# Node by node with four graphs innermost: another column order in a graph kernel on one core

## The chip, the cores and the metric

The kernel runs on one core of one Trainium2 chip. The metric is the device time of one execution in microseconds; lower is better.

## What is computed

64 graphs of 128 nodes with 128 features each go through two layers, each with a layer norm, a ReLU and a residual. The first layer has a convolution branch along the nodes (1 tap, then 17 taps), a message branch whose weights come from distances of three projected values, and a GRU-like gate over both. The second is a plain graph convolution. Cut to what matters:

```python
h = relu(layernorm(x))                                  # per node
c = relu(bn1(conv1(h)));  x_conv = relu(bn2(conv17(c)) + h)
s = h @ w_se.T + b_se                                   # 3 values a node
A = exp(-|s_n - s_m|^2) * adj
x_nmp = A @ relu(h @ w_msg.T + b_msg)
gi = [x_conv, x_nmp] @ w_ih.T + b_ih;  gh = h @ w_hh.T + b_hh
r, z = sigmoid(gi_r + gh_r), sigmoid(gi_z + gh_z)
x = x + (1 - z) * tanh(gi_n + r * gh_n) + z * h
x = x + adj @ (relu(layernorm(x)) @ weight) + bias
```

## The kernel before

The graphs are handled in 16 groups of four (`GG = 4`, `W = 512` columns), two groups being a pair (8 graphs, `CG`). Most of the first layer is kept transposed: features on the 128 partitions, and the 512 (node, graph) columns of a group along the free dimension. In those tiles (`hT`, `h_hi`, `h_lo`, `n_hi`, `n_lo`, `zh`, `cand`) the columns stand graph by graph, 128 nodes of one graph in a row. The nodes of a graph are loaded in an order by phase: `PH = 4` phases of `QN = 32` nodes, so that the convolution of 17 taps splits into products with inputs of one phase each.

`x_turn(g)` (L285) turns the four normalised graphs `hn` into PSUM with four transposes; ScalarE writes `h_hi` (rounded to fp32r) and `hT` from there, VectorE the rest `h_lo`. `conv1(g)` (L296) is one product of 512 columns, whose result ScalarE writes to `c1` (L567), laid out as [phase, graph of the pair, 36], two zeros at either end of the 32 nodes. `pre` (L756, on GpSimd) forms differences of phases in `ac` and `px` (a fast-convolution scheme with nine products in place of sixteen); ScalarE and VectorE split them into `cx_hi` (L537) and `cx_lo` (L862). `product` (L266) then runs, for each of the four or five taps `j` of one of nine inputs, three matmuls of 256 columns (`split_product`: L262, L263, L264) on `cx[:, x, :, j:j + QN]`, that is, eight runs of 32 numbers that start `j` numbers into a row of 36.

```python
last = split_product(acc[:, side * CG * QN:(side + 1) * CG * QN],
                     conv_hi[:, w * D:(w + 1) * D], conv_lo[:, w * D:(w + 1) * D],
                     cx_hi[:, x, :, j:j + QN], cx_lo[:, x, :, j:j + QN], ...)
```

`messages(g)` (L307) multiplies `hT` of one graph (the stationary operand) with `w_ms` (131 columns), after a bias matmul for each two graphs (L318); as an fp32 matmul each becomes two instructions at L320, with a weight load each. `neighbour_sums(g)` (L340) is for each graph the product of `msg` and `att`, again two instructions each. `gates_h`, `gates_n`, `gates_c` (L352 to L385) are 27 matmuls of 512 columns for each group. `o_turn(g)` (L390) turns the blend `zh` (stationary) back to nodes on partitions, in four transposes. The rest (`adj_h2`, `layer2`) works on nodes by partition.

Nothing is scheduled automatically. Every engine has its list of work written out: an `opening()`, and then `step(t)` for t = 1 to 8, in which TensorE alternates the parts for the two groups a, b of the next pair (turn, conv1, messages, distances, sums), the nine products of this pair, and the parts for the groups pp, qq of the pair before; then come the gates. A middle step begins with `x_turn(a)`, `o_turn(pp)`, the product of input `X22`, `conv1(a)` (which waits for `h_lo` of a), `messages(a)`, `x_turn(b)`, the product of `X12`, `o_turn(qq)`, `conv1(b)` (which waits for `h_lo` of b), `messages(b)`. In step 7 there is no next pair, so no `x_turn`, `conv1` and `messages`; step 8 has the last two groups' ends alone.

## Time and profile before

| | us |
|---|---|
| median of 3 runs (lowest, highest) | 382.32 (381.64, 383.23) |
| the profiled execution, whole time | 385.51 |
| its span in the profile | 383.4 |
| TensorE busy in the span | 345.2 |
| VectorE busy | 285.2 |
| ScalarE busy | 208.3 |
| GpSimd busy | 175.4 |

The span goes from the first to the last instruction of the core; the execution's whole time is 2.1 us more. In the rows below PE is TensorE's matmuls and PEld its weight loads, DVE is VectorE, ACT ScalarE, POOL GpSimd. A busy share counts the time in which an instruction of the engine is under way. Matmuls are pipelined: one starts before the last has ended, so their durations add to more than the time that passes, and what one costs the stream is read from start to start. In the timeline, equal instructions in a row are merged to one line with their number (x4), and the time in it is that of all of them.

### The profile page before, as it was taken

The page shows a single profiled execution, that of the slowest core. Times are in us where ns is not written, and L with a number is a line of the kernel's source. Part 1 is how long each engine was busy: PE and PEld are TensorE (multiplying, and loading weights), DVE is VectorE, ACT ScalarE, POOL GpSimd, SP SyncE. Part 2 cuts the span into 40 slices and gives each one's busy share as a digit, 9 for nine tenths or more (in the row PEclk, how much of TensorE's full clock was granted, in tenths as well). Part 3 has the DMA queues.
Part 4 walks back from the last instruction along what each step waited for, and adds up shares of the span by engine and source line. Part 5 has one row for each costly group of instructions (what it writes and reads, how often), then busy time and mean ns, then how long its engine had stood idle before and what let it go on. Part 6 is the DMA issues. An engine that isn't in the chain of part 4 may idle for free.

```text
span 383.4 us, 6302 instructions
## 1 busy us (share of the span) xinstructions
PE 345.2 (90%) x2196; PEld 314.9 (82%) x2196; DVE 285.2 (74%) x736; ACT 208.3 (54%) x402; POOL 175.4 (46%) x140
## 2 busy tenths in 40 slices
PE   7777956979999899999999999989999999989935
PEld 7776856759998899889987999889988998989725
DVE  3596878778877997698878887798758976743571
ACT  1545823485854586548745785458545835261422
POOL 7762336211890369224952298028901592153031
PEclk9875989998999999999999999999999999999955
DMA  7600020000130013000210031002100010000001
GB/s 257 264 3 0 0 85 0 0 3 0 57 109 2 1 41 122 6 0 30 100 39 1 2 110 56 0 2 68 44 1 2 0 57 0 3 29 27 0 0 56
DMA packets 7807, 15.10 MB, mean 39 GB/s; under 512 B 992, under 2 KB 1376, under 8 KB 7648
## 3 DMA queue, kind: packets, MB, share of 16 engines
q1 hardware_dynamic: 7488, 14.56, 10.9%
q8 instruction: 18, 0.29, 0.3%
q10 hardware_dynamic: 288, 0.14, 0.1%
q14 instruction: 13, 0.11, 0.1%
HBM read 10.50 MB, written 4.19 MB: 38 GB/s over the span
## 4 chain that ended last, share of the span: by engine, by line
issue 45%; POOL 32%; DVE 9%; PE 7%; ACT 5%; DMA 1%; SPq 0%; POOLq 0%; ACTq 0%; DVEq 0%
POOL work L1116 5%; POOL rs L1074 4%; POOL ac L769 3%; POOL base L1126 3%; POOL base L1128 3%; POOL px L773 3%; POOL base L1132 2%; POOL px L771 2%; POOL px L766 2%; POOL rs L1069 2%; DMA x_ring<-x_in 1%; ACT hn L548 1%; POOL px L763 1%; DVE cx_lo L862 1%; DVE st L786 1%
## 5 line engine op out<-in xcount | busy, mean ns | idle before, releaser
L1074 POOL TENSOR_TENSOR rs<-ve,neg_half 128x4 f32<-128x4 f32 x16 | 16.2, 1010 | 98.7 <-DVE ve L903 98.7
L262 PE MATMUL pP<-cx_hi,conv_hi 128*128 128x256 f32 x176 | 54.2, 308 | 4.1 <-DVE cx_lo L862 4.1
L264 PE MATMUL pP<-cx_hi,conv_lo 128*128 128x256 f32 x176 | 52.0, 296 | 0.0
L263 PE MATMUL pP<-cx_lo,conv_hi 128*128 128x256 f32 x176 | 52.0, 295 | 0.0
L262 PE MATMUL pQ<-cx_hi,conv_hi 128*128 128x256 f32 x144 | 46.0, 319 | 4.1 <-issue 3.6
L1069 POOL TENSOR_TENSOR rs<-ve,neg_half 128x8 f32<-128x8 f32 (+1 forms) x9 | 16.4, 1825 | 63.6 <-DVE ve L793 63.6
L263 PE MATMUL pQ<-cx_lo,conv_hi 128*128 128x256 f32 x144 | 43.2, 300 | 0.0
L264 PE MATMUL pQ<-cx_hi,conv_lo 128*128 128x256 f32 x144 | 43.2, 300 | 0.0
L262 PEld LDWEIGHTS pP<-cx_hi,conv_hi 128*128 128x128 f32 x176 | 34.1, 194 | 4.4 <-issue 2.5
L596 ACT ACTIVATE work<-work,nb,rs 128x128 f32<-128x128 f32 x64 | 26.3, 483 | 15.0 <-DVE nb L907 15.0
L862 DVE TENSOR_TENSOR cx_lo<-px,cx_hi 128x576 fp32r<-128x576 f32 x32 | 34.0, 1082 | 0.6 <-ACT cx_hi L537 0.6
L264 PEld LDWEIGHTS pP<-cx_hi,conv_lo 128*128 128x128 f32 x176 | 34.2, 194 | 0.0
L263 PEld LDWEIGHTS pP<-cx_lo,conv_hi 128*128 128x128 f32 x176 | 34.2, 194 | 0.0
L262 PEld LDWEIGHTS pQ<-cx_hi,conv_hi 128*128 128x128 f32 x144 | 28.9, 201 | 4.8 <-issue 3.7
L1116 POOL TENSOR_TENSOR work<-work,late 128x512 f32<-128x512 f32 x16 | 23.1, 1442 | 14.8 <-DVE pair L838 11.2
L263 PEld LDWEIGHTS pQ<-cx_lo,conv_hi 128*128 128x128 f32 x144 | 28.9, 201 | 0.0
L264 PEld LDWEIGHTS pQ<-cx_hi,conv_lo 128*128 128x128 f32 x144 | 28.9, 201 | 0.0
L923 DVE SCALAR_TENSOR_TENSOR xc_lo<-base,xc_hi 128x512 fp32r<-128x512 f32 x16 | 17.1, 1068 | 12.8 <-ACT xc_hi L606 12.8
L616 ACT ACTIVATE work<-pNR,rz_b 128x512 f32<-128x512 f32 x16 | 11.0, 687 | 26.4 <-PE pNR L264 26.4
L853 DVE TENSOR_TENSOR att<-att,adj_ring 128x512 f32<-128x512 f32 x16 | 23.6, 1474 | 1.7 <-ACT att L587 1.3
L548 ACT ACTIVATE hn<-x_ring,nb,rs 128x128 f32<-128x128 f32 x56 | 22.3, 483 | 1.6 <-DVE nb L799 1.6
L537 ACT ACTIVATE cx_hi<-px 128x576 fp32r<-128x576 f32 x32 | 20.8, 676 | 2.3 <-POOL px L763 2.3
(233 smaller groups left out, 1018.0 us busy)
## 6 DMA issues: line engine op xcount, KB each, us to landing
x_ring<-x_in SPq DMA_DIRECT2D x16, 256.0 KB, 2.6
adj_ring<-adj_in SPq DMA_DIRECT2D x16, 256.0 KB, 3.1
out<-x_ring SPq DMA_DIRECT2D x16, 256.0 KB, 2.0
work<-conv_in SPq DMA_DIRECT2D x1, 1088.0 KB, 7.7
x_ring<-gate_in SPq DMA_DIRECT2D x1, 576.0 KB, 8.0
work<-bias_in SPq DMA_DIRECT2D x1, 132.0 KB, 7.6
early<-early_in SPq DMA_DIRECT2D x1, 129.5 KB, 3.2
late<-late_in ACTq DMA_DIRECT2D x1, 128.0 KB, 3.4
```

Source lines behind the costliest of these rows:

```text
L262: pe.matmul(acc, w_hi, m_hi, start=start, stop=False)
L263: pe.matmul(acc, w_hi, m_lo, start=False, stop=False)
L264: return pe.matmul(acc, w_lo, m_hi, start=False, stop=stop)
L537: act.activation(cx_hi[:, CX_PARTS[k][0]:CX_PARTS[k][1]], cx_source(k), ACT.Copy).then_inc(cxhi_set, 1)
L548: last = act.activation(graph(hn[g % 2], j), xs(g, j), ACT.Identity, bias=nb1[:, i:i + 1], scale=rs1[:, i:i + 1])
L596: last = act.activation(graph(h2[g % 2], j), graph(x1[g % 2], j), ACT.Relu, bias=nb2[g % 2][:, j:j + 1], scale=rs2[g % 2][:, j:j + 1])
L853: dve.tensor_tensor(att[g % 2], att[g % 2], adjs(g), ALU.mult).then_inc(att_set, 1)
L862: dve.tensor_tensor(cx_lo[:, part], cx_source(k), cx_hi[:, part].bitcast(F32), ALU.subtract)\
L923: dve.scalar_tensor_tensor(xc_lo[:, 2 * e:2 * e + 2], base[e][:], 0.0, xc_hi[:, 2 * e:2 * e + 2].bitcast(F32), ALU.max, ALU.subtract)\
L1069: pool.tensor_tensor(rs1[:, lane], ve1[:, lane], neg_half[:, lane], ALU.pow).then_inc(rs1_set, 1)
L1074: pool.tensor_tensor(rs2[g % 2][:], ve2[g % 2][:], neg_half[:, 0:GG], ALU.pow).then_inc(rs2_set, 1)
L1116: pool.tensor_tensor(x1[g % 2].rearrange("p (g d) -> p g d", g=GG), x1[g % 2].rearrange("p (g d) -> p g d", g=GG), l1_bias, ALU.add).then_ ...
```

## The change

The columns of a group are kept node by node, with the four graphs innermost: column 4n + j is node n of graph j (`lane(t, j)` picks graph j in steps of four). `x_turn` and `neighbour_sums` write their results to PSUM in steps of four; `messages` and `o_turn` read their stationary operand in steps of four. `c1`, `ac`, `px`, `cx_hi`, `cx_lo` become [phase or input, group of the pair, 144], with the pads of eight numbers at either end, and a tap `j` starts `4 * j` numbers into the row, in two runs of 128. `xc_hi`, `xc_lo` and `base` hold each group's columns together. The order of the instructions and their number are the same on all engines.

```diff
--- before.py
+++ after.py
@@ -17,7 +17,8 @@
 TAPS = 17
 PH = 4
 QN = N // PH
-QP = QN + 4
+QW = QN * GG
+QR = (QN + 4) * GG
 EPS = 1e-5
 S = 3
 MS = D + S
@@ -94,17 +95,17 @@
         n_hi = [sb(f"n_hi{i}", [128, 2 * W], F32R) for i in range(2)]
         n_lo = [sb(f"n_lo{i}", [128, 2 * W], F32R) for i in range(2)]
 
-        c1 = sb("c1", [128, PH, CG, QP])
-        ac = sb("ac", [128, 2, CG, QP])
-        px = sb("px", [128, 8, CG, QP])
-        cx_hi = sb("cx_hi", [128, 9, CG, QP], F32R)
-        cx_lo = sb("cx_lo", [128, 9, CG, QP], F32R)
+        c1 = sb("c1", [128, PH, 2, QR])
+        ac = sb("ac", [128, 2, 2, QR])
+        px = sb("px", [128, 8, 2, QR])
+        cx_hi = sb("cx_hi", [128, 9, 2, QR], F32R)
+        cx_lo = sb("cx_lo", [128, 9, 2, QR], F32R)
         s22 = sb("s22", [128, CG * QN])
         s12 = sb("s12", [128, CG * QN])
         s32 = sb("s32", [128, CG * QN])
-        base = [sb(f"base{i}", [128, 2, CG, QN]) for i in range(2)]
-        xc_hi = sb("xc_hi", [128, PH, CG, QN], F32R)
-        xc_lo = sb("xc_lo", [128, PH, CG, QN], F32R)
+        base = [sb(f"base{i}", [128, 2, 2, QW]) for i in range(2)]
+        xc_hi = sb("xc_hi", [128, PH, 2, QW], F32R)
+        xc_lo = sb("xc_lo", [128, PH, 2, QW], F32R)
 
         sq = sb("sq", [128, GG, S])
         sv = sb("sv", [128, GG, S + 1])
@@ -188,6 +189,9 @@
 
         def graph(t, j):
             return t[:, j * N:(j + 1) * N]
+
+        def lane(t, j):
+            return t.rearrange("p (n g) -> p g n", g=GG)[:, j]
 
         def turn_bank(g):
             return pI if g == 1 else pF
@@ -267,7 +271,7 @@
                 for j, w in enumerate(weights):
                     last = split_product(acc[:, side * CG * QN:(side + 1) * CG * QN],
                                          conv_hi[:, w * D:(w + 1) * D], conv_lo[:, w * D:(w + 1) * D],
-                                         cx_hi[:, x, :, j:j + QN], cx_lo[:, x, :, j:j + QN],
+                                         cx_hi[:, x, :, j * GG:j * GG + QW], cx_lo[:, x, :, j * GG:j * GG + QW],
                                          start=j == 0, stop=j == len(weights) - 1)
                 return last
 
@@ -290,7 +294,7 @@
                 elif g > 1:
                     have(pe, hlo_set, g)
                 for j in range(GG):
-                    last = pe.transpose(graph(turn_bank(g), j), graph(hn[g % 2], j), ident[:])
+                    last = pe.transpose(lane(turn_bank(g)[:], j), graph(hn[g % 2], j), ident[:])
                 last.then_inc(hT_placed, 1)
 
             def conv1(g):
@@ -317,7 +321,7 @@
                 for i in range(2):
                     pe.matmul(ms[:, 2 * i:2 * i + 2, 0:MP], ones_r[:], bias_r[:], start=True, stop=False)
                     for j in range(2 * i, 2 * i + 2):
-                        last = pe.matmul(ms[:, j, 0:MS], graph(half(hT, g), j), w_ms, start=False, stop=j % 2 == 1)
+                        last = pe.matmul(ms[:, j, 0:MS], lane(half(hT, g), j), w_ms, start=False, stop=j % 2 == 1)
                 last.then_inc(ms_done, 1)
 
             def rows_turn(g):
@@ -346,7 +350,7 @@
                 elif g > 1:
                     have(pe, nlo_set, g)
                 for j in range(GG):
-                    last = pe.matmul(graph(rows_bank(g), j), graph(msg[g % 2], j), graph(att[g % 2], j), start=True, stop=True)
+                    last = pe.matmul(lane(rows_bank(g)[:], j), graph(msg[g % 2], j), graph(att[g % 2], j), start=True, stop=True)
                 last.then_inc(nmp_done, 1)
 
             def gates_h(g):
@@ -377,9 +381,7 @@
 
             def gates_c(g):
                 have(pe, xclo_set, g + 2 - g % 2)
-                j = slice(g % 2 * GG, (g % 2 + 1) * GG)
-                m_hi = xc_hi[:, :, j].rearrange("p k g m -> p g k m")
-                m_lo = xc_lo[:, :, j].rearrange("p k g m -> p g k m")
+                m_hi, m_lo = xc_hi[:, :, g % 2], xc_lo[:, :, g % 2]
                 gate_part(pR, 0, 0, m_hi, m_lo, False, True).then_inc(r_done, 1)
                 gate_part(pI[:], 0, 2, m_hi, m_lo, False, True).then_inc(i_done, 1)
                 gate_part(z_bank(g)[:], 0, 1, m_hi, m_lo, False, True).then_inc(z_done, 1)
@@ -395,7 +397,7 @@
                     have(pe, v_set, g + 1)
                 bank = pI if g % 2 else pH
                 for j in range(GG):
-                    last = pe.transpose(graph(bank, j), graph(zh[g % 2], j), ident[:])
+                    last = pe.transpose(graph(bank, j), lane(zh[g % 2], j), ident[:])
                 last.then_inc(o_placed, 1)
 
             def adj_h2(g):
@@ -563,9 +565,7 @@
                 if g % 2 == 0:
                     have(act, pre_set, 5 * (g // 2) - 2)
                     have(act, cxlo_set, 5 * (g // 2) - 4)
-                j = slice(g % 2 * GG, (g % 2 + 1) * GG)
-                act.activation(c1[:, :, j, 2:2 + QN].rearrange("p k g m -> p g k m"),
-                               conv1_bank(g)[:].rearrange("p (g k m) -> p g k m", g=GG, k=PH), ACT.Relu,
+                act.activation(c1[:, :, g % 2, 2 * GG:2 * GG + QW], conv1_bank(g)[:].rearrange("p (k w) -> p k w", k=PH), ACT.Relu,
                                bias=bn_b[:, 0:1], scale=bn_a[:, 0:1]).then_inc(c1_set, 1)
 
             def messages(g):
@@ -760,18 +760,18 @@
                 have(eng, pre_set, 5 * t + 3)
             have(eng, cxlo_set, 5 * t)
             if k == 1:
-                last = eng.tensor_tensor(px[:, X12:X21 + 1], c1[:, 1:3], c1[:, 3:4].to_broadcast([128, 2, CG, QP]),
+                last = eng.tensor_tensor(px[:, X12:X21 + 1], c1[:, 1:3], c1[:, 3:4].to_broadcast([128, 2, 2, QR]),
                                          ALU.subtract)
             elif k == 2:
-                last = eng.tensor_tensor(px[:, X32:X23 + 1, :, 0:QP - 1], c1[:, 0:3:2, :, 1:QP],
-                                         c1[:, 3:4, :, 0:QP - 1].to_broadcast([128, 2, CG, QP - 1]), ALU.subtract)
+                last = eng.tensor_tensor(px[:, X32:X23 + 1, :, 0:QR - GG], c1[:, 0:3:2, :, GG:QR],
+                                         c1[:, 3:4, :, 0:QR - GG].to_broadcast([128, 2, 2, QR - GG]), ALU.subtract)
             elif k == 3:
-                last = eng.tensor_tensor(ac[:], c1[:, 0:2], c1[:, 2:3].to_broadcast([128, 2, CG, QP]), ALU.subtract)
+                last = eng.tensor_tensor(ac[:], c1[:, 0:2], c1[:, 2:3].to_broadcast([128, 2, 2, QR]), ALU.subtract)
             elif k == 4:
                 last = eng.tensor_tensor(px[:, X11:X31 + 1], ac[:], px[:, X12:X32 + 1:2], ALU.subtract)
             else:
-                last = eng.tensor_tensor(px[:, X13:X33 + 1, :, 0:QP - 1], ac[:, :, :, 1:QP],
-                                         px[:, X12:X32 + 1:2, :, 0:QP - 1], ALU.subtract)
+                last = eng.tensor_tensor(px[:, X13:X33 + 1, :, 0:QR - GG], ac[:, :, :, GG:QR],
+                                         px[:, X12:X32 + 1:2, :, 0:QR - GG], ALU.subtract)
             last.then_inc(pre_set, 1)
 
         @block.vector
...
@@ -1117,7 +1117,7 @@
                                    l1_bias, ALU.add).then_inc(x1b_set, 1)
 
             def own(t, e):
-                phases = hT[t % 2][:].rearrange("p (g k m) -> p k g m", g=CG, k=PH)
+                phases = hT[t % 2][:].rearrange("p (h k w) -> p k h w", h=2, k=PH)
                 return phases[:, 2 * e:2 * e + 2]
 
             def sums(t):
...
```

## Rows read from the trace of the kernel before

**Rows 1.** The page: busy time by engine, and TensorE's granted clock in 40 slices.

```profile
PE 345.2 (90%) x2196; PEld 314.9 (82%) x2196; DVE 285.2 (74%) x736; ACT 208.3 (54%) x402; POOL 175.4 (46%) x140
...
PEclk9875989998999999999999999999999999999955
```

**Rows 2.** Busy time by stretch of the middle, with count, clock and DMA.

```profile
core 0: us, PE busy (x) PEld busy (x) DVE busy (x) ACT busy (x) POOL busy (x), PEclk, DMA share, GB/s
130.00:170.00 40.00, 38.82 (x263) 35.60 (x262) 33.19 (x88) 24.90 (x50) 20.98 (x14) 1.00 0.12 40
...
sum 200.00, PE 195.54 PEld 179.52 DVE 161.15 ACT 121.95 POOL 100.87; mean PE 39.11 PEld 35.90 DVE 32.23 ACT 24.39 POOL 20.17
```

**Rows 3.** TensorE's timeline in a middle step: `X12`, then `o_turn(qq)`, `conv1(b)`.

```profile
253.88 0.28 PE L263 MATMUL pP<-cx_lo,conv_hi 128*128 128x256 f32 x1
...
254.11 0.29 PE L262 MATMUL pP<-cx_hi,conv_hi 128*128 128x256 f32 x1
...
255.29 0.28 PE L262 MATMUL pP<-cx_hi,conv_hi 128*128 128x256 f32 x1
...
255.65 0.60 PE L398 MATMUL pI<-ident,work 128*128 128x128 f32 x4
256.57 0.50 PE L262 MATMUL pH<-h_hi,early_hi 128*128 128x512 f32 x1 [0.33 <-DVE h_lo L813]
```

**Rows 4.** TensorE's timeline: bias matmul and messages of a; gates on n, xc, next group.

```profile
252.19 0.28 PE L318 MATMUL pNR<-bias_r,ones_r 128*128 128x264 f32 x1
252.31 0.61 PE L320 MATMUL pNR<-early,hT 128*128 128x131 f32 x4
...
278.13 0.40 PE L262 MATMUL pNR<-n_hi,gate_hi 128*128 128x512 f32 x1
...
280.23 0.40 PE L262 MATMUL pNR<-xc_hi,gate_hi 128*128 128x512 f32 x1
...
282.33 0.39 PE L262 MATMUL pNR<-h_hi,gate_hi 128*128 128x512 f32 x1
```

**Rows 5.** The opening at the lower clock: stretch, then TensorE's product of `X21`.

```profile
33.00:36.00 3.00, 3.00 (x15) 3.00 (x15) 2.13 (x4) 2.25 (x7) 0.00 (x0) 0.50 0.00 0
...
33.60 0.41 PE L262 MATMUL pQ<-cx_hi,conv_hi 128*128 128x256 f32 x1
...
35.52 0.41 PE L262 MATMUL pQ<-cx_hi,conv_hi 128*128 128x256 f32 x1
```

**Rows 6.** Groups by shape (busy us, mean ns); L320 by itself (min/median/max); sums (timeline).

```profile
L262 PE MATMUL pP<-cx_hi,conv_hi 128*128 128x256 f32 x176 | 54.2, 308 | 4.1 <-DVE cx_lo L862 4.1
...
L262 PE MATMUL pQ<-cx_hi,conv_hi 128*128 128x256 f32 x144 | 46.0, 319 | 4.1 <-issue 3.6 <-DVE conv_lo L867 0.5
...
L320 PEld LDWEIGHTS pNR<-early,hT 128*128 128x128 f32 x128 | 18.6, 204 | 0.7
...
L398 PEld LDWEIGHTS pI<-ident,work 128*128 128x128 f32 x32 | 4.0, 151 | 3.2 <-DVE work L885 3.2
...
L320 PE MATMUL pNR<-early,hT x8: 273/275/275, 252.3 to 253.2; 128*128 128x131 f32 x8
...
272.07 1.06 PE L349 MATMUL pF<-att,msg 128*128 128x128 f32 x8
```

**Rows 7.** TensorE's timeline: two waits of the opening, and `conv1(a)` in a middle step.

```profile
20.09 0.36 PE L262 MATMUL pP<-cx_hi,conv_hi 128*128 128x256 f32 x1 [2.30 <-DVE cx_lo L862]
...
26.77 0.36 PE L262 MATMUL pP<-cx_hi,conv_hi 128*128 128x256 f32 x1 [1.76 <-DVE cx_lo L862]
...
250.29 0.28 PE L264 MATMUL pP<-cx_hi,conv_lo 128*128 128x256 f32 x1
251.41 0.47 PE L262 MATMUL pH<-h_hi,early_hi 128*128 128x512 f32 x1 [0.84 <-DVE h_lo L813]
```

**Rows 8.** Groups by shape of ScalarE and GpSimd that the change touches.

```profile
L567 ACT ACTIVATE c<-pH,bn_b,bn_a 128x512 f32<-128x512 f32 x15 | 11.7, 782 | 15.7 <-PE pH L264 15.7
...
L1126 POOL TENSOR_TENSOR base<-base,hT 128x512 f32<-128x512 f32 x8 | 13.0, 1623 | 13.0 <-DVE base L931 13.0
```

More of the change, by code:

```diff
@@ L917, in conv_out @@
                 have(dve, (sumE_set, sumO_set)[e], t + 1)
-                dve.scalar_tensor_tensor(base[e][:], (pQ, pP)[e][:].rearrange("p (s g m) -> p s g m", s=2, g=CG),
+                dve.scalar_tensor_tensor(base[e][:], (pQ, pP)[e][:].rearrange("p (s h w) -> p s h w", s=2, h=2),
                                          bn_a[:, 1:2], base[e][:], ALU.mult, ALU.add).then_inc(ct_set, 1)
@@ L930, in between @@
                 have(dve, xclo_set, 2 * t)
-                dve.scalar_tensor_tensor(base[1][:].rearrange("p s g m -> p s (g m)"),
+                dve.scalar_tensor_tensor(base[1][:].rearrange("p s h w -> p s (h w)"),
                                          pQ[:].rearrange("p (s w) -> p s w", s=2), bn_a[:, 1:2],
@@ L1057, in _ @@
             pool.memset(ones_r[:].bitcast(F32), 1.0).then_inc(rows_zero, 1)
-            pool.memset(px[:, X32:X23 + 1, :, QP - 1:QP], 0.0)
-            pool.memset(px[:, X13:X33 + 1, :, QP - 1:QP], 0.0)
+            pool.memset(px[:, X32:X23 + 1, :, QR - GG:QR], 0.0)
+            pool.memset(px[:, X13:X33 + 1, :, QR - GG:QR], 0.0)
             pool.memset(pair[:, 0, :, :, 1, S:S + 1], 1.0)
@@ L1127, in sums @@
                 pool.wait_ge(sum_half, 3 * t + 1)
-                pool.tensor_tensor(base[0][:].rearrange("p s g m -> p s (g m)"),
-                                   base[0][:].rearrange("p s g m -> p s (g m)"),
+                pool.tensor_tensor(base[0][:].rearrange("p s h w -> p s (h w)"),
+                                   base[0][:].rearrange("p s h w -> p s (h w)"),
                                    s12[:].unsqueeze(1).to_broadcast([128, 2, CG * QN]), ALU.add)\
@@ L1134, in sums @@
                 pool.wait_ge(s32_set, t + 1)
-                pool.tensor_tensor(base[1][:].rearrange("p s g m -> p s (g m)"),
-                                   base[1][:].rearrange("p s g m -> p s (g m)"),
+                pool.tensor_tensor(base[1][:].rearrange("p s h w -> p s (h w)"),
+                                   base[1][:].rearrange("p s h w -> p s (h w)"),
                                    s32[:].unsqueeze(1).to_broadcast([128, 2, CG * QN]), ALU.add)\
```

## The prediction

> **What bounds the kernel now.** First read the page's busy shares and granted clock. TensorE is busy 90% of the span, VectorE 74%, ScalarE 54%, GpSimd 46%, and TensorE's clock is at its full level of 2.4 GHz in nearly all of the middle [rows 1]. Then the busy time in five stretches of 40 us. TensorE is busy 39.1 us of each, VectorE 32.2, GpSimd 20.2, at granted clock 1.00 [rows 2]. A busy TensorE is not yet proof, since its matmuls overlap, so the third view is its timeline, and what the reader should look at there is starts, not durations. From one start to the next is what a matmul costs the stream. In a middle step I find two places where the spacing is larger than the work: `conv1(a)` starts 1.12 us after the last product matmul, against a usual 0.12, so 1.0 us is idle; `conv1(b)` starts 0.92 us after the turn of four, which needs 0.44, so 0.5 us is idle [rows 3, 7]. Both wait for `h_lo` from VectorE. Everything else in the step is TensorE's own pace, so what one of its instructions gains or loses outside these two places goes 1:1 into the span.
>
> **What paces a matmul.** The 512-column gate matmuls start 233 ns apart (18 in 4.20 us), the nine on `n` from one run, and also the nine on `xc` in runs of 32 [rows 4]. The 256-column products are of two kinds. Tap offset 0 (115 ns for the two starts shown) and offset 4 (120 ns: 255.65 - 255.29 over three) are quick; offsets 1, 2 and 3 take 131 ns (255.29 - 254.11 over nine) [rows 3]. The 264-column bias matmul takes 120 ns [rows 4]. Count the 16-byte pieces of SBUF that each reads in a partition: 128, 64, 72 (a run of 32 numbers that starts off a 16-byte boundary touches nine pieces, not eight) and 66. Divided (118 for the five starts of the quick kind), this is 1.82 to 1.84 ns a piece four times. At the lower clock level, 1.2 GHz, the same matmuls take 213 ns each at every offset [rows 5], which is 256 columns at 1.2 GHz and more than 72 x 1.82 = 131. The ninth piece vanishes there, so it isn't a fixed bubble of the array; it is the memory that delivers one piece in about 1.82 ns. All four are readings of the moving operand; that the law holds for the others is my step.
>
> The 128-column fp32 instructions are paced otherwise: from a merged line less its last instruction, 112 ns in the messages ((610 - 275) / 3), 109 in the turns ((600 - 273) / 3), 112 in the neighbour sums ((1060 - 275) / 7) [rows 3, 4, 6], where 32 pieces would need only 58. They use two array cycles a column, for stream and weights alike.
>
> **The change part by part.** No instruction is added, removed or moved on any engine; only patterns change.
>
> 1. Products (`cx_hi`, `cx_lo` at `j * GG`). Each now starts on a 16-byte boundary, in two runs of 128: 64 pieces at every tap, so 131 becomes 117 or 118 ns for offsets 1, 2, 3. These are 27 of the 40 taps of a step, by 3 matmuls, 81 of 120; the counts 3 x 176 + 3 x 144 = 960 confirm eight steps [rows 6]. The rows give 13 ns each, the law 8 x 1.82 = 14.5; I take 14. In steps 1 to 6, 18 of the 81 stand ahead of the two waits for `h_lo` and only lengthen them; 63 count, 378 in all. Step 7 has no `conv1`, all 81 count. In the opening the low clock and the waits leave some 45. Together 504 x 14 ns = -7.1 us. If all 648 counted it were -9.1.
>
> 2. Messages: the stationary operand `lane(hT, j)` steps by four fp32, one per 16-byte piece, so a weight load touches 128 pieces in place of 32. No row shows a stepped load. Lower bound: nothing, if the load port keeps up. Upper bound by the law above: 128 x 1.82 = 233 ns against 112, +121. I take the upper, since 1.82 was met by every operand that asked for pieces faster than that, and a load that needs a column every two cycles (0.83 ns) asks for one piece in each. There are 128 such loads [rows 6]; those of groups 0 and 1, 16 in all, stand ahead of waits of 2.30 and 1.76 us for `cx_lo` [rows 7] and are hidden, 112 count: +13.6, less some 0.5 where the first load of a row lies beside the bias matmul: +13.1 us.
>
> 3. Return turns `o_turn`: the stationary operand `zh` is stepped, 64 loads (32 on each of two banks [rows 6]), 109 to 233 ns, 0.5 us a group. In steps 1 to 6 they lie exactly ahead of the two waits for `h_lo`, whose makers don't need them: 0.5 into 1.0 + 0.12, and 0.5 into 0.5 + 0.12. They are hidden, unless `h_lo` comes sooner; then +6. In steps 7 and 8 nothing covers them: 4 groups, +2.0 us.
>
> 4. `x_turn` and neighbour sums write PSUM in steps of four. Lower bound nothing, upper the same 1.82 ns per element, 233 for 109 and 112. I take nothing: these instructions deliver a column in two array cycles, half the rate at which the 512-column matmuls write, so even a write of half speed has room.
>
> 5. The rest. ScalarE's `c1` (782 ns) writes runs of 128 in place of 32, and GpSimd's first sum with `own` (1623 ns) reads them [rows 8]; `pre` 2 and 5 shift by 16 bytes in place of 4. They may be a little quicker, or not, on engines that are busy 54% and 46% of the span [rows 1]. Vector work keeps its shapes. I cost all this at nothing: TensorE's own pace hides it, and if that cover were gone, 16 writes of `c1` at even 0.1 us either way would be 1.6 us.
>
> Sum: -7.1 + 13.1 + 2.0 = **+8.0 us**. The profiled execution took 385.5 us (span 383.4), 3.2 over the median of 382.3 of the three runs. The differences carry over, so from the median I get 390.3 us, and about 393.5 for a profiled execution like this one.
>
> **A rule beside the rows.** The Trainium skill (Advanced Engine Details and Errata, SBUF Cachelines) says SBUF has lines of 16 bytes, that two hits on a line are wanted to cover its latency and that a new line on each access is penalised; the 1.82 ns of the rows agree for the moving operand, and nothing here shows the stationary one. The same page (PSUM Cachelines) says that any non-contiguous pattern in PSUM slows matmuls significantly. No row shows one. By that rule part 4 has a price, which is the second rival below. The page TensorE: Matmul & The Clock Gate (LDWEIGHTS) lets a load take a time by its columns alone; by that, parts 2 and 3 are free and the first rival holds.
>
> **Rivals.**
> *Free steps (faster).* The weight port keeps up, as PSUM does. For it: loads lie beside the stream of the matmul before, and a load of 128 columns at 1.2 GHz asks far less bandwidth than the stream. Against it: it asks for a piece each 0.83 ns, and the ninth pieces weren't absorbed even though the queue could run ahead. Only -7.1 stays: 375.2 us, or 373 if all 648 count. It decides where a stepped load stays under about 165 ns; there 112 x 53 + 16 x 56 ns = 6.8 us eat the gain.
> *PSUM pays too (slower yet).* At 1.82 ns per element, 14 groups x 8 x 121 ns = 13.6 for the sums and 14 x 4 x 124 = 6.9 for the turns, which stand ahead of `h_lo`'s chain and aren't covered: 390.3 + 20.5 = 410.8 us. With free weights and slow PSUM it would be 395.7.
> *Half way.* Loads at some 155 to 180 ns: -7.1 + 112 x 43 to 68 ns + 16 x 46 to 71 ns, 380.8 to 384.0 us, no change that can be told.
> *The change doesn't do what it says*: the taps stay at 131 ns because of something other than alignment (a step of 36 between runs, say). Against it: offsets 0 and 4 have the same runs of 32 and the same step and are quick. That would give 382.3 + 15.1 = 397.4 us.
>
> **How the numbers follow.** Stepped loads at full price, PSUM free: 0.47, forecast 390.3 us, own range 386 to 394. Free steps 0.26, 373 to 377. PSUM pays with the loads 0.12, alone 0.05. Half way 0.06. Gain missing 0.04. The range 373.5 to 400 leaves out the two-fold price and little else. Faster by over 0.5% (about what a measurement of this kernel can tell from no change): 0.27. Within 0.5%: 0.06. Slower: 0.67.
>
> **What would show it.** Starts in the timeline of the changed kernel: products at 117 ns at each offset (part 1); the four message matmuls in a row 233 ns apart, their group of four merged at about 1.0 us in place of 0.61 (part 2); the `zh` turns likewise, with the wait for `h_lo` behind them shorter by the same (part 3); neighbour sums still 112 and `hn` turns 109 (part 4). If the messages stay at 112 my step from stream to weights was wrong and the kernel is faster; if the sums rise, the second rival holds.

## The result and the profile after

The changed kernel takes 387.36 us (383.32 to 389.76, 20 runs); the kernel before took 383.88 us (381.64 to 386.36, 20 runs) beside it. The ratio is 1.0063, with an interval of 1.0033 to 1.0092: slower by 0.6%, some 2.4 us. The forecast was slower by 8.0 us. Its direction holds, and its size doesn't. The ratio leaves out three runs of the changed kernel, over 1.5% above its fastest; the median of its other 17 is 386.25 us. The profiled executions agree with it: 388.15 us with a span of 386.0 after, 385.51 with 383.4 before, +2.65 us.

The page of the changed kernel, its busy time by engine and TensorE's granted clock, answers to [rows 1]:

```profile
PE 350.2 (91%) x2196; PEld 320.3 (83%) x2196; DVE 290.0 (75%) x736; ACT 208.8 (54%) x402; POOL 175.7 (46%) x140
...
PEclk9965969987999999999999999999999999999975
```

Busy time of the five stretches of the middle, the same ones as in [rows 2]:

```profile
130.00:170.00 40.00, 39.52 (x264) 36.45 (x263) 32.97 (x89) 25.35 (x50) 20.98 (x14) 1.00 0.12 40
...
sum 200.00, PE 196.91 PEld 182.02 DVE 163.21 ACT 121.33 POOL 100.85; mean PE 39.38 PEld 36.40 DVE 32.64 ACT 24.27 POOL 20.17
```

TensorE is busy 39.4 us of 40 in place of 39.1, still at granted clock 1.00. That tells nothing of the cause. The starts do. TensorE's timeline in a middle step, from `conv1(a)` to `conv1(b)`, answers to [rows 3, 4] and the last rows of [rows 7]:

```profile
253.54 0.47 PE L266 MATMUL pH<-h_hi,early_hi 128*128 128x512 f32 x1 [0.89 <-DVE h_lo L813]
...
254.42 1.09 PE L324 MATMUL pNR<-early,hT 128*128 128x131 f32 x4
...
257.18 0.28 PE L266 MATMUL pP<-cx_hi,conv_hi 128*128 128x256 f32 x1
...
258.25 0.29 PE L266 MATMUL pP<-cx_hi,conv_hi 128*128 128x256 f32 x1
...
258.62 0.66 PE L400 MATMUL pI<-ident,work 128*128 128x128 f32 x4
259.15 0.50 PE L266 MATMUL pH<-h_hi,early_hi 128*128 128x512 f32 x1
```

Four things are to be seen. A row of four message instructions takes 1.09 us where it took 0.61: less the last one's own 397 ns, (1090 - 397) / 3 = 231 ns from start to start, 112 before. The nine products at tap offsets 1 to 3 take (258.25 - 257.18) / 9 = 119 ns each, 131 before. The turn of four takes 0.66 us where it took 0.60, little more. And `conv1(b)` starts 0.53 us after the turn's start where it started 0.92 after it, with no idle time noted: most of the wait for `h_lo` there is gone. Some 0.1 us of it is left: the same part takes 0.41 in `e9` below.

Lines L324 and L400 by themselves (duration min/median/max in ns), after:

```profile
L324 PEld LDWEIGHTS pNR<-early,hT x80: 307/329/332, 129.6 to 302.8; 128*128 128x128 f32 x80
L400 PEld LDWEIGHTS pI<-ident,work x20: 202/212/220, 133.8 to 299.9; 128*128 128x128 f32 x20
```

and the messages' (two rows of four) and the return turn's before:

```profile
L320 PEld LDWEIGHTS pNR<-early,hT x8: 187/190/190, 252.2 to 253.1; 128*128 128x128 f32 x8
L398 PEld LDWEIGHTS pI<-ident,work x20: 141/142/142, 132.6 to 296.4; 128*128 128x128 f32 x20
```

The messages' weight load lasts 329 ns where it lasted 190; the turn's 212 for 142.

To see where the time went I laid the two timelines of TensorE side by side, part by part: both have the same parts in the same order. The length of a part is from its first start to the next part's first start. One middle step (step 4, from `x_turn(a)` to the next `x_turn(a)`):

| part | before | after | difference |
|---|---|---|---|
| `messages`, a and b | 1.14 + 1.13 | 2.09 + 2.09 | +1.91 |
| the products together | 16.93 | 15.97 | -0.95 |
| `o_turn(pp)` | 0.36 | 0.40 | +0.04 |
| `o_turn(qq)` to `conv1(b)`, wait included | 0.93 | 0.53 | -0.40 |
| `x_turn`, a and b | 0.80 | 0.80 | 0 |
| neighbour sums, two groups | 1.62 | 1.62 | 0 |
| gates | 12.59 | 12.59 | 0 |
| the whole step | 40.99 | 41.56 | +0.57 |

And the whole run, with the forecast's terms sorted by the same stages:

| stage | forecast | measured |
|---|---|---|
| opening, up to step 1 | -0.6 + 1.9 = +1.3 | -0.92 |
| steps 1 to 6 | +11.6 - 0.5 - 5.3 = +5.8 | +1.33 (step 1), 4 x 0.57 + 0.65 (step 6) = +2.93 |
| steps 7 and 8 | -1.1 + 2.0 = +0.9 | -0.69 |
| sum | +8.0 | +2.65 |

Step 1 isn't like the others in either trace, and its +1.33 isn't all the change's. Between 80 and 97 us the granted clock was 0.90 before and 0.80 after, and in the kernels below it was 0.80, 0.90 or 1.00, whatever the edit. In `e8` (below), at 0.80, step 1 took 45.50 us where before took 44.08, though each middle step of `e8` is 0.36 shorter; the changed kernel, at 0.80 as well, took 45.42. The opening and the last step vary too, whatever the edit: 76.7 to 79.1 us and 19.2 to 20.6 in the traces of all kernels here. So I compare middle steps, which repeat within 0.01 us in most kernels, and ratios over several runs.

### The profile page after: what moved, and what is told of

It reads as the page before. It is cut to its first block, busy times and chain, and to the rows that moved or that the text cites. A ratio compares the mean times of both kernels' runs of the same rounds, so it can differ in the third digit from the quotient of the medians.

```text
span 386.0 us, 6302 instructions
## 1 busy us (share of the span) xinstructions
PE 350.2 (91%) x2196; PEld 320.3 (83%) x2196; DVE 290.0 (75%) x736; ACT 208.8 (54%) x402; POOL 175.7 (46%) x140
## 4 chain that ended last, share of the span: by engine, by line
issue 44%; POOL 32%; DVE 10%; PE 7%; ACT 4%; DMA 1%; SPq 0%; POOLq 0%; ACTq 0%; DVEq 0%
POOL work L1116 5%; POOL rs L1074 4%; POOL ac L769 3%; POOL base L1126 3%; POOL base L1128 3%; POOL px L773 3%; POOL px L771 2%; POOL base L1132 2%; POOL px L766 2%; POOL rs L1069 2%; POOL px L763 2%; ACT hn L550 1%; DMA x_ring<-x_in 1%; DVE conv_lo L867 1%; DVE cx_lo L862 1%
## 5 line engine op out<-in xcount | busy, mean ns | idle before, releaser
L268 PE MATMUL pP<-cx_hi,conv_lo 128*128 128x256 f32 x176 | 50.9, 289 | 0.0
L267 PE MATMUL pP<-cx_lo,conv_hi 128*128 128x256 f32 x176 | 50.8, 289 | 0.0
L266 PE MATMUL pQ<-cx_hi,conv_hi 128*128 128x256 f32 x144 | 45.1, 313 | 2.4 <-issue 1.9
L268 PE MATMUL pQ<-cx_hi,conv_lo 128*128 128x256 f32 x144 | 42.2, 293 | 0.0
L862 DVE TENSOR_TENSOR cx_lo<-px,cx_hi 128x576 fp32r<-128x576 f32 x32 | 35.0, 1115 | 0.6 <-ACT cx_hi L539 0.6
L324 PE MATMUL pNR<-early,hT 128*128 128x131 f32 x128 | 34.1, 397 | 0.0
L324 PEld LDWEIGHTS pNR<-early,hT 128*128 128x128 f32 x128 | 32.4, 325 | 0.6
L1116 POOL TENSOR_TENSOR work<-work,late 128x512 f32<-128x512 f32 x16 | 21.8, 1362 | 17.2 <-DVE pair L838 13.6
L853 DVE TENSOR_TENSOR att<-att,adj_ring 128x512 f32<-128x512 f32 x16 | 25.5, 1596 | 3.6 <-ACT att L587 3.5
L923 DVE SCALAR_TENSOR_TENSOR xc_lo<-base,xc_hi 128x512 fp32r<-128x512 f32 x16 | 18.5, 1159 | 12.1 <-ACT xc_hi L606 12.1
```

The lines of the kernel that those rows point to most:

```text
L266: pe.matmul(acc, w_hi, m_hi, start=start, stop=False)
L267: pe.matmul(acc, w_hi, m_lo, start=False, stop=False)
L268: return pe.matmul(acc, w_lo, m_hi, start=False, stop=stop)
L324: last = pe.matmul(ms[:, j, 0:MS], lane(half(hT, g), j), w_ms, start=False, stop=j % 2 == 1)
L853: dve.tensor_tensor(att[g % 2], att[g % 2], adjs(g), ALU.mult).then_inc(att_set, 1)
L862: dve.tensor_tensor(cx_lo[:, part], cx_source(k), cx_hi[:, part].bitcast(F32), ALU.subtract)\
```

## The experiments

The theory after the first comparison: the stepped weight load costs 233 ns, as forecast, but half a microsecond of each step's first longer group of messages is taken up by the wait of `conv1(b)`; the turns' stepped load is nearly free for a reason not yet known. The rival to the part on the wait: the wait went because `h_lo(b)` comes sooner by itself (longer runs, another layout), and the messages' price is paid in full elsewhere. Short diffs are against the changed kernel or the kernel before, as said. The middle steps of all of them stand together here, read as above, as medians of steps 2 to 5 (for `e6` the steps are 40.2 to 40.4):

| kernel | messages of a group | `o_turn(qq)` to `conv1(b)` | products | step | ratio to before (interval) |
|---|---|---|---|---|---|
| before | 1.13 | 0.93 | 16.93 | 40.99 | 1 |
| after | 2.09 | 0.53 | 15.97 | 41.56 | 1.0063 (1.0033 to 1.0092) |
| `e1` after, messages read plainly | 1.13 | 1.03 | 15.95 | 40.20 | 0.9872 (0.9832 to 0.9911) |
| `e4` after, with a plain copy | 1.13 | 1.14 | 15.94 | 40.30 | 0.9918 (0.9889 to 0.9948) |
| `e5` before, messages stepped | 2.09 | 0.42 | 16.91 | 42.37 | 1.0230 (1.0205 to 1.0255) |
| `e6` before, taps on boundaries | 1.13 | 1.03 | 16.01 | 40.2 | 0.9875 (0.9845 to 0.9905) |
| `e7` `e4`, ScalarE's order changed | 1.13 | 0.81 | 15.95 | 39.97 | 0.9887 (0.9853 to 0.9921) |
| `e8` before, ScalarE's order changed | 1.13 | 0.57 | 16.92 | 40.63 | 0.9966 (0.9934 to 0.9998) |
| `e9` after, ScalarE's order changed | 2.09 | 0.41 | 15.96 | 41.44 | 1.0078 (1.0047 to 1.0109) |

### The messages alone: e1 and e5

From the changed kernel, the messages' stationary operand as 128 numbers in a row again:

```diff
-                        last = pe.matmul(ms[:, j, 0:MS], lane(half(hT, g), j), w_ms, start=False, stop=j % 2 == 1)
+                        last = pe.matmul(ms[:, j, 0:MS], graph(half(hT, g), j), w_ms, start=False, stop=j % 2 == 1)
```

> The changed kernel with one edit: the messages load 128 neighbouring columns of hT as the stationary operand, not one graph in steps of four (so the messages mix the graphs; everything else is as in the change). Theory A (a stepped load costs the messages 233 ns for 112, and the wait of conv1(b) for h_lo gives back some 0.5 us of it in each middle step): the L324 spacing returns to 112 ns, a messages group from 2.09 to 1.13 us, conv1(b) waits 0.5 us again, the step falls from 41.56 to about 40.2 us, the span from 386.0 to about 377, the ratio to before about 0.984. Theory B (the cost of the change lies elsewhere, in the PSUM writes or the return turns): the time stays within 1 us of the changed kernel's.

Measured: 378.33 us (376.12 to 381.31, 6 runs), 0.9872 of before. The messages are back at their old rows, and so is the wait. TensorE's timeline of `e1`:

```profile
249.31 0.66 PE L400 MATMUL pI<-ident,work 128*128 128x128 f32 x4
250.35 0.50 PE L266 MATMUL pH<-h_hi,early_hi 128*128 128x512 f32 x1 [0.38 <-DVE h_lo L813]
...
251.27 0.61 PE L324 MATMUL pNR<-early,hT 128*128 128x131 f32 x4
```

`conv1(b)` starts 1.04 us after the turn in place of 0.53. A step is 1.36 us shorter: -1.90 from two groups of messages, +0.50 from the wait, and 0.04 elsewhere.

The same single edit on the kernel before:

```diff
+        def lane(t, j):
+            return t.rearrange("p (n g) -> p g n", g=GG)[:, j]
...
-                        last = pe.matmul(ms[:, j, 0:MS], graph(half(hT, g), j), w_ms, start=False, stop=j % 2 == 1)
+                        last = pe.matmul(ms[:, j, 0:MS], lane(half(hT, g), j), w_ms, start=False, stop=j % 2 == 1)
```

> The kernel before with one edit: the messages load their stationary operand in steps of four (mixing the graphs), all else as before. Theory A: L320 at 233 ns, each messages group 0.95 us longer, of which the wait of conv1(b) for h_lo takes back 0.5 us in each middle step: step 41.0 to 42.4 us, the whole 382.3 + 8 to 9 = some 391.5, ratio 1.021 to 1.025. My prediction's reckoning without the absorbed wait: + 13, ratio 1.034.

Measured: 392.15 us (391.47 to 393.22, 5 runs), 1.023 of before, +8.8 us. A step is 1.38 us longer: 1.90 less 0.51 at `conv1(b)`. So the wait goes with the messages' step alone, in the old layout too: the rival, a sooner `h_lo` by the new layout, is out. The waits view shows it by kernel (matmul and what it waited for: us in total, times, longest). Before, then `e5`, then `e1`:

```profile
PE pH L262 <- DVE h_lo L813: 8.8, 11, 3.1
```

```profile
PE pH L265 <- DVE h_lo L816: 7.4, 6, 3.1
```

```profile
PE pH L266 <- DVE h_lo L813: 10.5, 12, 3.1
```

With stepped messages five of eleven waits for `h_lo` are no longer noted, those of steps 2 to 6 (step 1 had none at `conv1(b)`); the changed kernel has 6 as well.

### The products alone: e6

The kernel before, with each tap's window moved to the boundary below; the shapes are the same:

```diff
-                                         cx_hi[:, x, :, j:j + QN], cx_lo[:, x, :, j:j + QN],
+                                         cx_hi[:, x, :, j // 4 * 4:j // 4 * 4 + QN], cx_lo[:, x, :, j // 4 * 4:j // 4 * 4 + QN],
```

> The kernel before with one edit: every tap's window starts on a 16-byte boundary (offset 0 for taps 0 to 3, 4 for tap 4), so the convolution adds the wrong neighbours; layout and runs of 32 as before. Theory A (pieces of 16 bytes pace the products): 117 to 119 ns at every tap, 9-matmul stretches 0.11 us shorter, 0.8 us a step where no wait stands behind, -6 to -7 us in all, ratio 0.982 to 0.985. Rival (the runs of 128, not the boundary, made the products of the change quick): 131 ns stays, ratio 1.00.

Measured: 379.24 us (376.78 to 382.46, 6 runs), 0.9875 of before. All taps are now 117 to 121 ns apart, in eight runs of 32 numbers as before, so it was the alignment, and not the short runs by themselves (`e3` has the long ones off the boundary). The products save 0.91 us a step, and some 0.1 of it goes into a longer wait at `conv1(b)` (1.03 for 0.93): the gain of the product of `X12` stands ahead of that wait, as the prediction had it. In the middle steps the two edits add: 1.38 us more by `e5` and 0.78 less by `e6` are +0.60, and the change measured +0.57. As ratios, 0.9875 and 1.0230 add to +1.05% where the change measured +0.63%; with each ratio uncertain by 0.3%, that difference can't be told from none.

### Why conv1(b) waited: e8 and e9

The prediction took the 0.5 us idle ahead of `conv1(b)` for a wait that starts with `x_turn(b)`, so that whatever moves `x_turn(b)` moves the wait's end with it. The trace of before tells another story, in rows I hadn't read. The timeline of all engines, kernel before, around `x_turn(b)`:

```profile
130.34 0.60 PE L293 MATMUL pF<-ident,hn 128*128 128x128 f32 x4
...
130.98 0.17 DVE L903 TENSOR_SCALAR ve<-mv 128x4 f32<-128x4 f32 x1
131.06 0.16 DVE L821 COPY sv<-pNR 128x12 f32<-128x12 f32 x1
...
131.25 0.60 ACT L574 ACTIVATE msg<-pNR 128x512 f32<-128x512 f32 x1 [1.06 <-DVE sv L821]
...
131.75 0.59 ACT L554 ACTIVATE h_hi<-pF 128x512 fp32r<-128x512 f32 x1
...
132.86 0.69 DVE L813 SCALAR_TENSOR_TENSOR h_lo<-pF,h_hi 128x512 fp32r<-128x512 f32 x1 [0.26 <-ACT hT L556]
...
133.61 0.50 PE L262 MATMUL pH<-h_hi,early_hi 128*128 128x512 f32 x1 [0.33 <-DVE h_lo L813]
```

`h_hi(b)` starts 1.41 us after the turn, though the turn's result is there much sooner. Ahead of it in ScalarE's list stands the ReLU of `messages(a)` (L574), which sat idle 1.06 us for VectorE's little copy `sv` (L821); and that one stands behind VectorE's normalisation of another group (L903). So what ended the wait was a time set by VectorE. TensorE could lose half a microsecond ahead of it at no cost. In the changed kernel the same rows:

```profile
131.69 0.60 PE L297 MATMUL pF<-ident,hn 128*128 128x128 f32 x4
131.89 0.17 DVE L821 COPY sv<-pNR 128x12 f32<-128x12 f32 x1 [0.35 <-PE pNR L324]
...
132.10 0.60 ACT L574 ACTIVATE msg<-pNR 128x512 f32<-128x512 f32 x1 [1.51 <-DVE sv L821]
...
132.59 0.59 ACT L556 ACTIVATE h_hi<-pF 128x512 fp32r<-128x512 f32 x1
...
133.71 0.69 DVE L813 SCALAR_TENSOR_TENSOR h_lo<-pF,h_hi 128x512 fp32r<-128x512 f32 x1 [0.28 <-ACT hT L558]
...
134.45 0.50 PE L266 MATMUL pH<-h_hi,early_hi 128*128 128x512 f32 x1
```

Now `sv` waits for TensorE's messages, and `h_hi(b)` follows the turn by 0.90 us. `h_lo(b)` ends at 134.40, and `conv1(b)` starts 0.05 later, as it did before (133.55 and 133.61): it is still the last thing waited for, but TensorE would be there only some 0.1 us sooner by itself. To show it by an edit, ScalarE's two parts change places in the kernel before:

```diff
-                    messages(a)
                     hidden(b)
+                    messages(a)
```

> The kernel before with one edit: on ScalarE in each step hidden(b) stands ahead of messages(a). Theory: the stretch from o_turn(qq) to conv1(b) falls from 0.93 us to 0.6 or 0.44, 0.3 to 0.5 us a step, ratio 0.992 to 0.995. Rival (conv1(b) waits for x_turn(b)): 0.93 us and ratio 1.00.

Measured: 381.64 us (379.29 to 384.92, 12 runs), 0.9966 of before. The timeline of `e8`:

```profile
131.83 0.60 PE L293 MATMUL pF<-ident,hn 128*128 128x128 f32 x4
...
132.47 0.60 ACT L554 ACTIVATE h_hi<-pF 128x512 fp32r<-128x512 f32 x1 [0.79 <-PE pF L293]
...
133.44 0.60 ACT L574 ACTIVATE msg<-pNR 128x512 f32<-128x512 f32 x1
```

`h_hi(b)` starts 0.64 us after the turn, released by the turn itself, and the part up to `conv1(b)` falls from 0.93 to 0.57: the order of ScalarE made 0.36 of the 0.5 us wait. The step is shorter by just that, 40.63 for 40.99. Five such steps are 1.8 us, a ratio of 0.995; the measured 0.9966 has an interval that holds it, but is above the 0.992 to 0.995 expected, so the steps show the effect and the whole time barely does.

The same exchange in the changed kernel, where theory says that the wait is filled by the messages already:

> The changed kernel with the one edit of the reordered ScalarE list (hidden(b) ahead of messages(a)). In the changed kernel the wait behind o_turn(qq) is gone, since the longer messages cover it. Theory: the edit that gave 0.35 us a step to the kernel before gives nothing here, 0.53 us from o_turn(qq) to conv1(b) as without, ratio to before 1.004 to 1.009. Rival (the edit helps in some other way): 0.3 us a step, ratio 0.998 to 1.002.

Measured: 386.05 us (384.66 to 388.60, 10 runs), 1.0078 of before (1.0047 to 1.0109), against 1.0063 without the exchange: no gain to be told. The part falls from 0.53 to 0.41 and the step by 0.12, where 0.53 was expected to stay: the messages had covered the wait up to this 0.12. The same edit is worth three times as much where the wait is still there.

### What a stepped weight load costs: e2 and e10

The changed kernel with the messages' and the return turns' stationary operands in steps of 1, 2, 3 or 4 numbers, by the group's number:

```diff
+        def stepped(t, g, j):
+            s = g % 4 + 1
+            first = {1: j * N, 2: j // 2 * 2 * N + j % 2, 3: j * 16, 4: j}[s]
+            return t[:, first:first + (N - 1) * s + 1:s]
...
-                        last = pe.matmul(ms[:, j, 0:MS], lane(half(hT, g), j), w_ms, start=False, stop=j % 2 == 1)
+                        last = pe.matmul(ms[:, j, 0:MS], stepped(half(hT, g), g, j), w_ms, start=False, stop=j % 2 == 1)
...
-                    last = pe.transpose(graph(bank, j), lane(zh[g % 2], j), ident[:])
+                    last = pe.transpose(graph(bank, j), stepped(zh[g % 2], g, j), ident[:])
```

> The changed kernel, a probe: the stationary operands of the messages and of the return turns are read in steps of 1, 2, 3 and 4 numbers for groups with g mod 4 = 0, 1, 2, 3 (so the graphs are mixed). What counts is the spacing of the four merged instructions. If a load costs 1.82 ns for each 16-byte piece it touches (32, 64, 96, 128 pieces), the messages stand 112, 117, 175 and 233 ns apart; if any step costs the full price, 112, 233, 233, 233. The return turns took 120 ns at step 4 in the changed kernel: if they pay half price for a piece (0.91 ns, as each number is read once there and twice for an fp32 matmul), they take 109, 109, 109 and 120; then the messages' law is 2 x 0.91 ns.

One run, 380.28 us. The timeline of `e2`, one row of four messages at each step size, 1 to 4 in this order, and ahead of the last a return turn, of group 7 and so at step 4:

```profile
166.98 0.61 PE L329 MATMUL pNR<-early,hT 128*128 128x131 f32 x4
...
172.16 0.63 PE L329 MATMUL pNR<-early,hT 128*128 128x131 f32 x4
...
207.22 0.85 PE L329 MATMUL pNR<-early,hT 128*128 128x131 f32 x4
...
210.94 0.66 PE L405 MATMUL pI<-ident,work 128*128 128x128 f32 x4
...
212.39 1.09 PE L329 MATMUL pNR<-early,hT 128*128 128x131 f32 x4
```

From start to start (medians over the middle): 112, 118, 175 and 233 ns. A load of 128 numbers touches 32, 64, 96 and 128 pieces of 16 bytes; the last three are 1.84, 1.82 and 1.82 ns a piece, and the first lies on the floor of 112 ns that the instruction has anyway. The law from the moving operand gives the right times for the messages' weights. At steps of 1 to 4 the pieces touched grow just as the length of the stretch that is read, so these runs can't tell which of the two is paid for; a step above 4 would, and none was tried. The Trainium skill (TensorE: Matmul & The Clock Gate, LDWEIGHTS) has a load take its number of columns over 1.2 GHz and names no step, which for 128 columns makes an estimate of 107 ns. The spacing at step 1, 112 ns, is near that; at step 4, 233 ns, it is over twice that, and the measurement decides.

The return turns don't follow it, nor the 109, 109, 109 and 120 expected: 109 ns at step 1, 117 to 125 at step 2, 112 to 117 at step 3, 121 to 130 at step 4. Step sizes 1 and 3 fall to `o_turn(pp)`, 2 and 4 to `o_turn(qq)`, so place and step size aren't separated here.

Is 1.82 ns a matter of fp32 matmuls, which take two instructions each? The changed kernel with the convolution's fp32r weights loaded in steps of four, sixteen taps of the seventeen:

```diff
+        def of_four(t, w):
+            block = w // 4 * 4 if w < T16 else M22 + (w - M22) // 4 * 4
+            first = block * D + w - block
+            return t[:, w * D:(w + 1) * D] if w == T16 else t[:, first:first + 4 * (D - 1) + 1:4]
...
-                                         conv_hi[:, w * D:(w + 1) * D], conv_lo[:, w * D:(w + 1) * D],
+                                         of_four(conv_hi, w), of_four(conv_lo, w),
```

> The changed kernel, a probe: the products load their convolution weights (fp32r, the stationary operand) in steps of four numbers from the block of the four taps, save the 17th tap, which stays plain (so the taps are mixed). It asks why a stepped load takes 233 ns in the fp32 messages and no more than 122 in the return turns. If the price belongs to the load port (1.82 ns for each of 128 pieces), the products rise from 118 to 233 ns and the kernel by some 90 us. If it comes from fp32 matmuls, whose load reads each number twice at 0.91 ns, a single reading of 128 pieces takes 117 and the products stay at 117 to 125 ns; the kernel stays within a few us.

One run, 466.39 us. The timeline of `e10`, a product's second to fifth tap, the fifth the plain one, and what follows it:

```profile
202.75 0.40 PE L271 MATMUL pQ<-cx_hi,conv_hi 128*128 128x256 f32 x1
...
204.88 0.29 PE L271 MATMUL pQ<-cx_hi,conv_hi 128*128 128x256 f32 x1
...
205.24 0.39 PE L346 MATMUL pF<-right,left 128*128 128x512 f32 x1
```

(204.88 - 202.75) / 9 = 237 ns for a stepped one, (205.24 - 204.88) / 3 = 120 for a plain one. So an fp32r matmul pays about the same for its load as an fp32 one: 128 pieces at 1.82 are 233. What is left as the exception among the loads is the transpose.

### Off the boundary in long runs: e3

The changed kernel with the taps `j` numbers in, not `4 * j`, and `conv1` reading `h_lo` as moving operand in steps of four:

```diff
-                                         cx_hi[:, x, :, j * GG:j * GG + QW], cx_lo[:, x, :, j * GG:j * GG + QW],
+                                         cx_hi[:, x, :, j:j + QW], cx_lo[:, x, :, j:j + QW],
...
+                              half(h_hi, g).rearrange("p (g n) -> p g n", g=GG), half(h_lo, g).rearrange("p (n g) -> p g n", g=GG), True, True)\
```

> The changed kernel, a probe with two edits: tap j starts j numbers into the row (not 4 j), so taps 1, 2, 3 start off a 16-byte boundary in two runs of 128; and the second matmul of conv1 reads h_lo in steps of four numbers (512 pieces in place of 128). Both give wrong sums. By the law of 16-byte pieces the products at offsets 1 to 3 read 66 pieces and take 120 ns, against 117 to 119 at offsets 0 and 4 and 131 in the kernel before (72 pieces); if a start off the boundary costs by itself, 131. The stepped matmul of conv1 takes 512 x 1.82 = 932 ns in place of 232, if the law holds for stepped moving operands.

One run, 389.72 us. The timeline of `e3`, nine matmuls at offsets 1 to 3, then `conv1`:

```profile
252.35 0.28 PE L266 MATMUL pP<-cx_hi,conv_hi 128*128 128x256 f32 x1
...
253.44 0.28 PE L266 MATMUL pP<-cx_hi,conv_hi 128*128 128x256 f32 x1
...
255.14 0.62 PE L267 MATMUL pH<-h_lo,early_hi 128*128 128x512 f32 x1
255.58 0.42 PE L268 MATMUL pH<-h_hi,early_lo 128*128 128x512 f32 x1
```

The products are (253.44 - 252.35) / 9 = 121 ns apart, though off the boundary: two runs have 33 pieces each, 66 x 1.82 = 120. By offset they are 122, 125 and 118 ns on average over steps 2 to 5, so the law gives the mean and not each offset. The 131 ns of the kernel before need both, the offset and many short runs. The stepped `h_lo` took 255.58 - 255.14 = 440 ns for 512 numbers, each in a piece of its own: 0.86 ns a number. The law said 932. So 1.82 ns isn't the price of a piece for the moving operand in general; it fits there where most pieces are read whole.

### A version that beats both: e4 and e7

The changed kernel keeps the products' gain; the messages get a plain copy. ScalarE copies `hT` graph by graph into `hn`, which is free by then, and the messages load from there:

```diff
-                        last = pe.matmul(ms[:, j, 0:MS], lane(half(hT, g), j), w_ms, start=False, stop=j % 2 == 1)
+                        last = pe.matmul(ms[:, j, 0:MS], graph(hn[g % 2], j), w_ms, start=False, stop=j % 2 == 1)
...
+                have(act, hT_set, g + 1)
+                act.activation(hn[g % 2][:].rearrange("p (g n) -> p g n", g=GG),
+                               half(hT, g).rearrange("p (n g) -> p g n", g=GG), ACT.Copy).then_inc(plain_set, 1)
```

> The changed kernel, all of the computation kept: ScalarE copies hT graph by graph into the tile hn of the same group, free by then, and the messages load their stationary operand from there. 16 more ScalarE instructions. Theory A: PE as in the run with plain messages, messages 1.13 us a group, if the copy (0.6 to 1.1 us, it reads in steps of four) is done when conv1 is; the time then 376 to 379 us, ratio to before 0.98 to 0.99. Rival: the copy stands ahead of candidate(qq) and conv1_out(a) on ScalarE and delays the chain to h_lo(b), so that conv1(b) waits 0.5 to 1.1 us more a step: ratio 0.99 to 1.0.

Measured: 380.28 us (378.41 to 383.22, 12 runs), 0.9918 of before. The copy's line in `e4`:

```profile
L562 ACT ACTIVATE hn<-hT x16: 1121/1130/1159, 10.4 to 291.8; 128x512 f32<-128x512 f32 x16
```

TensorE's timeline of `e4`, the return turn and `conv1(b)`:

```profile
251.21 0.66 PE L401 MATMUL pI<-ident,work 128*128 128x128 f32 x4
252.35 0.50 PE L267 MATMUL pH<-h_hi,early_hi 128*128 128x512 f32 x1 [0.49 <-DVE h_lo L818]
```

The wait is 0.1 us longer than in `e1` (1.14 for 1.04 from the turn), and so is the step: sixteen copies of 1.13 us, 18 us on ScalarE, cost TensorE no more than that in steps 2 to 5. In step 6 the part takes 1.54 us where it takes 0.96 in `e1`, and over the whole run the ratios, 0.9918 and 0.9872, are 1.8 us apart, with intervals that overlap. The ratio lies just above the 0.98 to 0.99 expected, in the rival's range, but by less of a wait in the middle than the rival's 0.5 to 1.1 us. With the exchange of `e8` put in as well, `hidden(b)` ahead of `messages(a)` and the copies in a function of their own (`plain`), that of b behind both:

```diff
+                    plain(a)
...
-                    messages(a)
                     hidden(b)
+                    messages(a)
+                    plain(b)
```

> The version with plain copies for the messages (all of the computation kept), and on ScalarE in each step hidden(b) ahead of messages(a), the copy for b behind it. Theory: conv1(b) waits for h_lo(b) because h_hi(b) stands behind the message ReLU of a, which waits for VectorE's normalisation. Then the wait behind o_turn(qq), 1.10 us from its start to conv1(b), shrinks by 0.3 to 0.6, to the moment when VectorE is through with the pairs of a; 6 steps give 2 to 3.5 us, ratio to before 0.983 to 0.987 against 0.992 without. If the wait comes from x_turn(b) itself, as my prediction had it, nothing changes.

Measured: 379.23 us (376.81 to 379.75, 6 runs), 0.9887 of before (0.9853 to 0.9921). The step is 39.97, 0.33 under `e4`, within the 0.3 to 0.6 expected of the wait; the ratio is above the 0.983 to 0.987 expected, and the intervals of `e4` and `e7` overlap. Both are faster than either kernel, by 0.8% and 1.1% than the one before.

## Why the prediction was right or wrong

**Messages: the price right, its share on the path wrong.** 233 ns was forecast, and 231 to 233 measured; the half-way and the free rivals are out. But "so what one of its instructions gains or loses outside these two places goes 1:1 into the span" failed. The messages of a stand outside the two waits and yet ahead of one of them, and I took for granted that the second wait's end moves with the stream, because `h_lo(b)` is made from `x_turn(b)`. It was set by VectorE, through ScalarE's order. 0.51 us of `messages(a)` was absorbed in each of steps 2 to 5 and 0.43 in step 6 (`e5`), some 2.5 us in all; in step 1 `conv1(b)` didn't wait in either kernel. In the change it is 0.40 and 0.32, since the turn ahead is itself 0.04 longer and 0.1 of the wait is left. The rows that tell it were in the trace of before: at each wait, follow the maker back by one more step on its own engine.

**Groups 2 and 3, +1.9 us, cost next to nothing.** They stand in the opening; the messages of group 2 are still +0.95 us there, but the wait behind those of group 3, ahead of the product of `X11`, falls from 3.57 to 1.88 us. In `e5`, where the messages alone differ from before, `conv1(2)` starts 0.80 us sooner than before and that product 0.60 sooner, so both groups together moved it by 0.2. I had looked for waits behind groups 0 and 1 alone.

**Return turns: the load mis-sized.** `o_turn` was put at 233 ns by the law. It took 118 to 130, on average 120 in `o_turn(pp)` and 124 in `o_turn(qq)`. The two turns in step 7 cost 0.03 and 0.05 us in place of 1.0, and those of step 8 nothing at all: their part, 7.97 us long with its waits for VectorE, has the same length in both kernels. +2.0 was forecast, +0.1 came. "That the law holds for the others is my step" was the weak place, for this operand only.

**Products: about right in the steps.** 117 to 121 ns at every tap, about as forecast, and some 12.6 ns saved where I took 14. In a step this makes 0.95 us by parts against 63 x 14 = 0.88: fewer ns each, but the nine of `X12` are in the sum too (72 x 12.6 = 0.91, and 0.04 in `X22`), since little of the wait behind them is left. The opening was to give 0.6; together with groups 2 and 3 it stands at -0.9. But 2.0 us were gained before `conv1(0)`, in `e5` just as here, and partly lost again behind it, and behind `X11` the two kernels ran at different granted clocks (0.83 before and 0.66 after between 50 and 60 us, 0.83 and 1.00 in the next ten). So the opening's share of the products stays open. Step 7 gave 0.78 where 1.1 was forecast: its first `adj` part waits for ScalarE, and that wait takes the gain of the products ahead of it (-0.24, then +0.15 in the part that ends with the wait). Timeline of before:

```profile
337.03 1.16 PE L405 MATMUL pZ<-adj_ring,work 128*128 128x128 f32 x8 [1.25 <-ACT work L596]
```

**PSUM in steps of four: free, as taken.** Neighbour sums 112 ns before and 111 after, turns of `hn` 109 and 109; the parts of the step have equal lengths. The rival that PSUM pays, 410.8 us, is out. The Trainium skill (Advanced Engine Details and Errata, PSUM Cachelines) says that any non-contiguous pattern slows matmuls significantly; for these 128-column fp32 instructions the trace shows nothing of the kind. Whether it holds for 512-column fp32r matmuls (233 ns for 512 columns, against 112 for 128 here) wasn't tried.

**The sum.** Over steps 1 to 6, with one middle step as the measure: forecast 16 x 0.121 = +1.94 for messages, -0.88 for products and -0.08 for the bias's cover, +0.97; measured +1.91 - 0.95 + 0.04 - 0.40 = +0.60, and -0.03 in all the other parts together, +0.57. The miss in the step is the wait: what TensorE gained or lost ahead of `conv1(b)` did not go 1:1 into the span. Of the 5.3 us between forecast and traces, 1.5 are in steps 1 to 6, 1.6 in steps 7 and 8 (the return turns, at 0.1 in place of 2.0, less 0.3 that the products gave too little), and 2.2 in the opening, where +1.9 for groups 2 and 3 was priced in full ahead of a wait and the rest isn't split. No one step of the prediction makes the whole miss. The direction came out as forecast through the messages' load. Part of the size is chance, since the opening alone varies by up to 2.4 us between traces.

## What to carry to other kernels

Choose a layout by all its readers: what makes the moving operand's runs long and aligned may put every number of a weight load in a 16-byte piece of its own, and the load then paces the matmul (here 233 ns in place of 112). Where both are wanted, a plain copy on an engine with slack is cheaper (here 1.13 us of ScalarE for 0.95 us of TensorE saved, at 0.1 us a middle step for two of them, and 0.6 in step 6). And before a cost goes 1:1 into the span, ask of the next wait behind it what ends it: an engine's order of work may have put a fixed time there, and it takes up what comes ahead.
